# Sample 2's x loaded once and turned on TensorE, with new orders in the first steps of an adapter and linear kernel

## The reference, cut to what matters

```python
def _L0_cond_ref(hidden_states, language_ids, W1, b1, W2, b2, gamma, beta):
    w1 = W1[language_ids]                      # 512 x 128
    w2 = W2[language_ids]                      # 128 x 512
    h = jax.nn.relu(jnp.einsum('bsh,bha->bsa', hidden_states, w1) + b1[language_ids][:, None, :])
    adapted = jnp.einsum('bsa,bah->bsh', h, w2) + b2[language_ids][:, None, :]
    x = hidden_states + adapted
    mean = jnp.mean(x, axis=-1, keepdims=True)
    var = jnp.mean(jnp.square(x - mean), axis=-1, keepdims=True)
    normed = (x - mean) * jax.lax.rsqrt(var + LN_EPS)
    return normed * gamma[language_ids][:, None, :] + beta[language_ids][:, None, :]
...
x = x + _L0_cond_ref(x, itok_B_0_8, ...)
x = x + (jnp.einsum('bti,bio->bto', x, W[itok_B_0_30]) + b[itok_B_0_30][:, None, :])
```

## Time and profile before

| | |
|---|---|
| median of three runs | 611.79 us (609.99 to 613.36) |
| the profiled execution's own time | 614.65 us |
| its span, first to last instruction | 612.8 us |
| busy PE, POOL, DVE, ACT | 601.9, 559.4, 525.1, 522.1 us |
| moved by DMA | 166.23 MB, mean 271 GB/s |
| chain that ended last | PE 86%, DMA 4%, SP's queue 4% |
| PE start of down(1), down(2), down(3) | 24.81, 46.67, 67.86 us |

### The profile page before, as it was taken

One profiled execution on the slowest core, in us unless ns is written; L12 is line 12 of the kernel. 1 busy time (PEld: TensorE's weight loads), 2 busy tenths in 40 slices (PEclk: granted clock), 3 DMA queues, 4 the chain that ended last, 5 costly groups with the idle time before them and its releaser, 6 DMA issues.

```text
span 612.8 us, 10739 instructions
## 1 busy us (share of the span) xinstructions
PE 601.9 (98%) x2891; PEld 495.3 (81%) x2891; DVE 525.1 (86%) x1151; ACT 522.1 (85%) x770; POOL 559.4 (91%) x263
## 2 busy tenths in 40 slices
PE   9879999999999999999999999999999999999998
PEld 7657787888888888888888888888888888888887
DVE  1769988898998899999889899889899889899673
ACT  4867889998888989888989888989889989888770
POOL 5757899999999999999999999999999999999830
PEclk9998999999999999999999999999999999999999
DMA  9999999999999999999999999999999999997222
GB/s 297 282 271 230 267 290 275 325 298 283 302 274 274 322 300 260 303 279 299 281 295 252 306 282 293 280 312 264 295 277 286 287 312 269 296 290 266 86 87 103
DMA packets 125939, 166.23 MB, mean 271 GB/s; under 512 B 11062, under 2 KB 72768, under 8 KB 121812
## 3 DMA queue, kind: packets, MB, share of 16 engines
q1 hardware_dynamic: 125524, 165.32, 96.2%
q10 hardware_dynamic: 288, 0.52, 0.3%
q0 software_dynamic: 96, 0.05, 0.0%
HBM read 132.17 MB, written 33.55 MB: 270 GB/s over the span
## 4 chain that ended last, share of the span: by engine, by line
PE 86%; DMA 4%; SPq 4%; DVE 2%; issue 2%; ACT 2%; DVEq 0%; ACTq 0%
PE o_bank L830 18%; PE o_bank L832 18%; PE o_bank L831 17%; PE n_bank L848 8%; PE d_bank L832 6%; PE d_bank L830 6%; PE d_bank L831 6%; PE y_bank L830 2%; PE y_bank L832 2%; PE y_bank L831 2%; DMA out<-out_half 2%; SPq L251 2%; DMA x_quad<-in_x 1%; DMA w_raw<-in_L_cond_W 1%; ACT x_tok L550 1%
## 5 line engine op out<-in xcount | busy, mean ns | idle before, releaser
L830 PE MATMUL o_bank<-w_hi,x1T_hi 128*128 128x512 f32 x512 | 205.7, 402 | 1.2 <-DVE x1T_lo L723 1.2
L832 PE MATMUL o_bank<-w_hi,x1T_lo 128*128 128x512 f32 x512 | 200.2, 391 | 0.0
L831 PE MATMUL o_bank<-w_lo,x1T_hi 128*128 128x512 f32 x512 | 199.2, 389 | 0.0
L441 POOL TENSOR_TENSOR w_lo<-w_raw,w_hi 128x1024 fp32r<-128x1024 f32 x62 | 147.8, 2408 | 10.2 <-ACT w_hi L524 10.2
L514 ACT ACTIVATE norm<-y,neg_mean_rstd,rstd 128x512 f32<-128x512 f32 x128 | 153.0, 1271 | 1.1 <-DVE neg_mean_rstd L708 1.1
L436 POOL TENSOR_TENSOR x_tok<-x_tok,b_bc 128x1024 f32<-128x1024 f32 x60 | 143.9, 2422 | 10.0 <-DMA b_bc<-in_L_cond_b 9.8
L407 POOL TENSOR_TENSOR xs_lo<-xT,xs_hi 128x2048 fp32r<-128x2048 f32 x28 | 129.5, 4624 | 1.4 <-ACT xs_hi L566 0.5
L658 DVE STREAM_TRANSPOSE xT<-x_quad 128x512 f32<-128x512 f32 x120 | 126.9, 1099 | 3.1 <-DMA x_quad<-in_x 3.1
L550 ACT ACTIVATE x_tok<-y,neg_mean 128x512 f32<-128x512 f32 x128 | 91.5, 717 | 33.6 <-DVE neg_mean L678 33.6
L830 PEld LDWEIGHTS o_bank<-w_hi,x1T_hi 128*128 128x128 f32 x512 | 96.3, 188 | 22.9 <-issue 2.8
L735 DVE TENSOR_TENSOR out_half<-o_bank,b_bc 128x512 f32<-128x512 f32 x127 | 86.9, 685 | 32.3 <-PE o_bank L832 30.8
(11 more groups left out here) (93 smaller groups left out, 825.1 us busy)
## 6 DMA issues: line engine op xcount, KB each, us to landing
w_raw<-in_L_cond_W SPq DMA_DIRECT2D x32, 1024.0 KB, 7.3
out<-out_half SPq DMA_DIRECT2D x63, 512.0 KB, 7.8
x_tok<-in_x SPq DMA_DIRECT2D x31, 1024.0 KB, 9.5
x_quad<-in_x SPq DMA_DIRECT2D x120, 256.0 KB, 8.3
w_raw<-in_L_cond_W SPq DMA_DIRECT2D x64, 256.0 KB, 4.0
b_bc<-in_L_cond_b SPq DMA_DIRECT2D x64, 256.0 KB, 7.5
x_tok<-in_x ACTq DMA_DIRECT2D x2, 256.0 KB, 3.4
x_tok<-in_x SPq DMA_DIRECT2D x2, 256.0 KB, 4.1
```

Source lines behind the costliest of these rows:

```text
L441: pool.tensor_tensor(w_lo[q][:, c:c + 2, :], w_raw[q][:, c:c + 2, :], w_hi[q][:, c:c + 2, :].bitcast(F32), ALU.subtract).then_inc(w_lo_don ...
L830: pe.matmul(acc, lhs_hi, rhs_hi, start=first, stop=False)
L831: pe.matmul(acc, lhs_hi, rhs_lo, start=False, stop=False)
L832: return pe.matmul(acc, lhs_lo, rhs_hi, start=False, stop=last)
```

## The change

Sample 2's x is loaded once, into the two tiles of `out_half`, whose first outputs are not written before step 2. PE turns it from there into four free banks (`turn_third_x`, 16 transposes), and DVE copies these to `xT[2]` (`copy_third_xT`). POOL's add of b2 for sample 2 reads `out_half` and writes `x_tok[0]`. `x_quad[0]` is free for sample 4, and the first outputs wait until POOL has read. The zeros of `keep_clock` move to `y`, the ten matmuls in step 1 go. The rest are orders: up(2) runs whole ahead of the pair; b2 moves ahead in SP's steps 1 and 2; ACT makes W2's high part of sample 2 after `norm`, then relu, then W's, and W2's of sample 3 at the end of step 2; POOL adds b2 first, then the identity; DVE makes the statistics of sample 1 ahead of the last two `low_x1` and leaves three of sample 3's four transpositions to the end of step 2.

```diff
@@ sync @@
-                if loads:
+                if loads and k.since(2):
                     sp.wait_ge(sq_done, k.count(NT, 0, 0))
                     load_x(k.sample(-1), q)
...
+                if loads and not k.since(2):
+                    sp.wait_ge(x_b2_done, NT)
+                    load_b2(lang, q)
                 if loads:
                     if k.since(2):
                         sp.wait_ge(x1_lo_done, k.count(NC, 1, 0))
                     load_params(lang, (k.x + 1) % 3)
+                if k.last(2):
+                    sp.wait_ge(x_b2_done, k.count(NT, 0, NT))
+                    load_b2(lang, q)
                 if quads:
...
-            load_x_quads(2, 0)
+            for half in range(2):
+                sp.dma_start(out_half[half][:, :, :], x_rows[2, :, 2 * half:2 * half + 2, :]).then_inc(x2_in, 16)
@@ gpsimd @@
                     if t == 0:
-                        pool.wait_ge(x_in[p], 16 * k.pairs(0) + 16)
+                        if k.last(2):
+                            pool.wait_ge(sq_done, NT)
+                            pool.wait_ge(x2_in, 32)
+                        else:
+                            pool.wait_ge(x_in[p], 16 * (k.pairs(0) if p == 0 else k.pairs(-2)))
...
-                    pool.tensor_tensor(pair, pair, b2_of(k)[:, :].rearrange("p (o h) -> p o h", o=1
+                    pool.tensor_tensor(pair, out_half[t // 2][:, :, :] if k.last(2) else pair, b2_of(k)[:, :].rearrange("p (o h) -> p o h", o=1
...
+                    if k.last(2):
+                        plus_identity()
+                        low_w2(p, k.count(1, 0, 1))
+                    elif follow:
                         low_w2(q, k.count(1, -1, 1))
@@ scalar @@
-                if follow:
+                if k.last(2):
+                    high_w2_of_next(Step(0, 1))
+                    relu(k)
+                elif follow:
                     high_w2_of_next(k)
@@ vector @@
+                    if k.last(2):
+                        dve.wait_ge(x_b2_done, 2 * NT + t + 2)
                     dve.wait_ge(stored[t // 2], k.count(16, 2, STORE_CREDIT))
...
+            def copy_third_xT(c):
+                dve.wait_ge(first_xT_turned, 2 * NC + c + 1)
+                dve.tensor_copy(xT[2][:, c, :], third_xT_bank(c)[:, :]).then_inc(xT_done, 1)
@@ tensor @@
+                    if k.last(1) and t == NT - 1:
+                        pe.wait_ge(xT_done, 2 * NC + 1)
...
+            def turn_third_x(c):
+                if c == 0:
+                    pe.wait_ge(x2_in, 32)
+                    pe.wait_ge(y_done, NT)
+                for t in range(NT):
+                    ins = pe.transpose(third_xT_bank(c)[:, t * P:(t + 1) * P], out_half[t // 2][:, t % 2, c::NC], ident[:, :])
+                ins.then_inc(first_xT_turned, 1)
...
             up_in_float32(k1, 0, NC)
-            keep_clock(10, o_bank[1])
+            for c in range(NC):
+                turn_third_x(c)
             down(k1)
+            pe.wait_ge(xT_done, 3 * NC)
             for c in range(NC):
                 turn_norm(k1, c)
-            up_in_float32(Step(0, 2), 0, 2)
+            up_in_float32(Step(0, 2), 0, NC)
```

More of the change, by code:

```diff
@@ L139, in adapter_then_conditional_linear @@
         param_rows = norm[0:L, :, :]
-        zeros = out_half[1][:, 1, 0:P]
+        zeros = y[:, 0, 0:P]
         param_table = sb("param_table", [P, L, NP])
@@ L157, in first_xT_bank, with x2_tile, third_xT_bank @@
             return [*n_bank, *o_bank][c]
+        def x2_tile(t):
+            return out_half[t // 2][:, t % 2, :]
+        def third_xT_bank(c):
+            return [d_bank[0], *o_bank, n_bank[0]][c]
         def norm_bank(k, c):
@@ L188, in adapter_then_conditional_linear @@
         xq_in = [sem(f"xq_in{i}") for i in range(2)]
+        x2_in = sem("x2_in")
         x_in = [sem(f"x_in{i}") for i in range(2)]
@@ L325, in step @@
                     store(k, 2, 0)
-                if loads:
+                if loads and k.since(3):
                     sp.wait_ge(x_b2_done, k.count(NT, 0, NT))
@@ L462, in step @@
                 else:
-                    if turn:
+                    if turn and not k.last(2):
                         plus_identity()
@@ L475, in step @@
                         low_xs(k)
-                if follow and not k.since(2):
+                if k.last(2):
                     low_w2(q, k.count(1, -1, 1))
@@ L576, in step @@
                 high_w(k, 2)
-                if adapter:
+                if adapter and not k.last(2):
                     relu(k)
@@ L589, in step @@
                 high_x1(k, 3)
+                if k.last(2):
+                    high_w2_of_next(k)
             act.dma_start(x_tok[0][:, 1, :], x_rows[0, :, 1, :]).then_inc(first_x_in[1], 16)
@@ L623, in _ @@
             square(k1, 3)
+            deviation(k1)
             high_x1(k1, 2)
             high_x1(k1, 3)
-            deviation(k1)
-            high_w2_of_next(k1)
             for p in range(2, 2 + ROUND):
@@ L656, in turn_next_x @@
                 if c == 0:
-                    dve.wait_ge(xq_in[1 - k.b], 16 * NQ * k.pairs(-1))
+                    dve.wait_ge(xq_in[1 - k.b], 16 * NQ * (k.pairs(1) if k.b else k.pairs(-1)))
                 dve.transpose(xT[(k.x + 1) % 3][:, c, :].rearrange("p (b j) -> p b j", j=SQ),
@@ L743, in step @@
                     turn_next_x(k, 0)
-                    turn_next_x(k, 1)
                     low_h(k)
@@ L774, in step @@
                 if k.last(2):
+                    turn_next_x(k, 1)
                     turn_next_x(k, 2)
                     turn_next_x(k, 3)
+            def copy_third_xT(c):
+                dve.wait_ge(first_xT_turned, 2 * NC + c + 1)
+                dve.tensor_copy(xT[2][:, c, :], third_xT_bank(c)[:, :]).then_inc(xT_done, 1)
             k0, k1 = Step(0, 0), Step(0, 1)
@@ L789, in _ @@
             inverse_deviation(k0)
-            turn_next_x(k1, 0)
+            copy_third_xT(0)
             low_h(k1)
-            turn_next_x(k1, 1)
+            for c in range(1, NC):
+                copy_third_xT(c)
             y_pair(k1, 0)
@@ L800, in _ @@
             x1(k1, 3)
+            variance(k1)
+            inverse_deviation(k1)
             low_x1(k1, 2)
             low_x1(k1, 3)
-            variance(k1)
-            inverse_deviation(k1)
-            turn_next_x(k1, 2)
-            turn_next_x(k1, 3)
             for p in range(2, 2 + ROUND):
@@ L920, in step @@
                     linear_tile(k, 1)
-                if k.last(2):
-                    up_in_float32(k, 2, NC)
-                elif k.last(3):
+                if k.last(3):
                     up_in_float32(k, 0, NC)
-                else:
+                elif not k.last(2):
                     up(k)
```

## The result

The changed kernel takes **606.78 us** (median of 7 runs, 606.53 to 609.15); the kernel before on the same chip took 611.97 (7 runs, 609.99 to 613.36). The ratio is 0.9926, with a 95% interval of 0.9907 to 0.9944, so the change saves 5.2 us by the medians. I had predicted 604.7 in a range of 602.3 to 609.3: the sign, the place and the range hold; the size of the saving was 7.1 in the forecast. The two unchanged kernels were run in two more groups, where the medians differ by 3.3 and 5.2 us, so the saving is 3.3 to 5.2.

What follows compares the result with a forecast made beforehand. PE's work bounds the kernel, so only its waits can be saved. Terms -1.9 -4.0 -1.4 +0.5 +0.5 -0.8 sum to -7.1 us, from the median 611.79 to 604.7 us, range 602.3 to 609.3.

Steps and rivals of the forecast that it cites:

- -1.9 for turn_norm(2,0): PE's start: down(1) at 23.0 instead of 24.81, the pair ends at 36.8, so turn_norm(2,0) starts there, not at 38.70: -1.9 us.
- -4.0 for the stall: PE's wait before down(2) goes, since ACT does relu before sample 3's W2; down(2) comes at 40.5: -4.0 us.
- -1.4 for the half clock: The 1.2 GHz clock on PE from 46.6 to 49.4, after the stall before down(2), goes with it: -1.4 us.
- The second rival: In step 1 the clock falls on the transposes, down(1) takes 1.4 us more; total 606.1 us, chance 0.07.
- +0.5 at step 3: DVE has x1T_lo of chunk 2 at 49.3, PE wants it at 48.4; the wait of 0.40 becomes 0.9: +0.5 us.
- +0.5 at step 4: Three transpositions instead of two precede step 3's output on DVE; PE falls back from 6.9 to 6.4 us ahead: +0.5, bounds 0 and 1.1.
- The store: DVE's 1.17 us wait for a store at 87.64 and PE's 0.82 at 94.80 go: -0.8 us, bounds 0 and -1.1.
- The base: The 7.1 us saving from the profiled execution's 614.65 gives 607.5; the same saving from the median 611.79 gives 604.7 us.
- The cover on POOL: POOL's slack before up(4) reads xs_lo shrinks from 5.6 to about 3.6 us; cost 0.
- The rival's mechanism: DVE's output(2,0) waits for POOL's add and that for b2; each us b2 lands after 33.8 costs one; slower, chance 0.04.
- x2 late: Sample 2's x lands at 23.1 as the quads did, down(1) starts at 25.5; total 607.2 us, chance 0.10.
- Gain handed back: In the loop transfers or POOL carry the time, so only 1.05 MB less to move stays, 3.9 us; 607.9, chance 0.10.

Runs made afterwards that it cites:

- half_up: Changed kernel with up(2) again in two halves around the pair of linear tiles; 608.63 us, ratio 0.9940 to the kernel before.
- relu_late: Changed kernel with ACT's old order in step 2: W2's high half of sample 3 and w's high parts ahead of relu; 609.18 us, ratio 0.9944.
- Early_turn: Changed kernel with DVE's first two transpositions of sample 3's x ahead of output 0 in step 2; 605.76 us, and 605.41 us when repeated.
- b2_last: Changed kernel with sample 2's b2 issued behind the four x_quad loads of step 1; 608.82 us, ratio 0.9956 to the kernel before.
- extra_mb: Changed kernel plus a 1 MB load in step 1 that nobody reads, which step 2's quads wait for; 607.66 us, ratio 0.9924.
- early_both: Changed kernel with two transpositions ahead of output 0 and each step's second store ahead of the x_tok load; 605.8 us once, 622.2 to 648.2 in five executions.

## Why the prediction was right, and where it was off

**The terms of the start.** -1.9 for turn_norm(2,0): forecast 36.8, came at 36.67, and half_up gives 1.5 of it back. Its first part, down(1) 1.9 us earlier, is read from the traces alone: no run puts the x_quad load back. -4.0 for the stall: it went, and down(2) came at 40.40 where 40.5 was forecast; relu_late brings 2.2 of it back by one order. -1.4 for the half clock: down(2) runs at 1.00. The way to the stall was misread in one number: "ACT waits 6.30 us on the chain" is the time of that W2 from its issue at 35.87 to its landing. ACT itself was busy with `norm` until 38.6 and stood 3.6 us; the cause and the 4.0 us of PE do not change.

These were sized by one execution. The three traces of before put stalls and half clock at 8.5, 6.5 and 8.4 us together, in changing shares.

**x2 and the transpositions.** No wait for x2, 16 transposes in 2.0 us to 22.7, the copy 0.69 as its nearest row, down(1) at 22.95 for 23.0: right. But "at these rates 1.05 MB takes 5.5 or 2.6 us" rested on 189 GB/s as the rate of small pieces, and x2 in small pieces ran at 302. It held up because x2 landed at about 19 in rows of 2 KB; in small pieces it would still have come at 20.5, at the edge of the need. The second rival, with the clock falling on transposes, falls: 1.00 throughout. The Trainium skill ("TensorE: Matmul & The Clock Gate", Part 4: PE-mode transpose) says that they do not count as busy in the same way as other matmuls; these 2.0 us do not bear it out here, which does not test a longer stretch.

**What is late next.** +0.5 at step 3: 0.76 at 49.15 where 0.9 was forecast at 48.4 to 49.3. +0.5 at step 4: 0.31 at 68.86. Early_turn removes both in its first trace.

**The store, the step that failed.** "I take the wait as gone, -0.8, with bounds 0 and -1.1." It isn't the change that removes it: the second and third traces of before lack it, the second of after has 1.48 us of it, moved to 63.45, and there it costs 1.6 us of wait more than 0.31 and 1.7 of half clock. The bound should have reached to +3.3.

**The base, the other step that failed.** "That execution is 2.86 above the median of the runs, to which the same saving gives 604.7." An execution that lies above its median does so by stalls, and stalls are what the change removes; so the same saving can't be taken from the median. With the means of three traces a side the saving is 5.3, and 611.79 less 5.3 is 606.5. The second group, with 3.3, shows how far this still moves.

**The range.** Its ends do not follow from the parts it names: 603 and 607.9, each widened by 1.8, give 601.2 and 609.7, not 602.3 and 609.3. The measured time lies inside either.

**POOL and b2.** The cover on POOL held: idle 5.73 us before w2_lo at 49.08, xs_lo(4) from 63.82. b2 landed at 29.2, 31.3 and 27.7 in the three traces where 29.6 was forecast; in the second POOL waited 0.21 us for it, until 31.48. Sample 3's quads were forecast near 31: in the first trace the last was issued at 24.8 and took at least 9.4 us, so it came at 34.2 or later. That cost nothing, since DVE takes them up at 37.47, but it is the risk that early_turn runs into. The rival's mechanism (DVE blocked by POOL's adds) was not seen, and its deciding point was put at 33.8 on the path through DVE; a shorter one through POOL's identity and ACT's w decides near 31.8. This is an estimate from b2_last: 33.0 less the 1.2 us that it cost.

**The rivals.** x2 late and clock lost: not borne out. Gain handed back: not by transferring or POOL, as extra_mb shows, but in part by the store wait of the second trace.

## What to carry to other kernels

Before a saving is taken from the profile, ask which of its stalls every execution has: two or three traces of the same kernel cost little, and the sum "span less waits less half the time at half clock" tells at once whether they differ by anything else. A saving made of stalls is compared with the mean stalls, not subtracted from the median as it is. And a queue's own waits have a place: in early_both, moving one load behind a wait of the issuing engine cost 16 to 42 us in five of six executions, against the sixth, though the same bytes moved.

## What was not expected of the hardware

- Issuing the four x_quad loads of one step (at 36 to 42 us) took SP 6.66, 8.15 and 3.76 us in the three traces of the changed kernel and 8.97, 7.72 and 3.62 in those of the kernel before.
- The granted clock does not follow from the length of a wait alone. It fell to 0.50 with or after waits of 4.04, 3.58, 3.08, 1.90 and 1.76 us (the last in early_both, which also has falls with 3.19 and 2.23), and stayed at 1.00 after waits of 2.16 and 1.81 (relu_late), 1.81 (before, third), 1.74 (before, first) and 1.73 us (b2_last), and after one of 2.76 in early_both at 294.75. In the second trace of the changed kernel it fell half a microsecond after PE had started again:

```profile
70.91 0.45 PE L864 MATMUL o_bank<-w_lo,x1T_hi 128*128 128x512 f32 x1
71.15 0.63 PE L865 MATMUL o_bank<-w_hi,x1T_lo 128*128 128x512 f32 x1
...
74.55 0.39 PE L864 MATMUL o_bank<-w_lo,x1T_hi 128*128 128x512 f32 x1
```

- Small pieces cost a fifth of the rate (302 against 379 GB/s), while the x_quad loads, with pieces as small, ran at half of it.
